# Routing inside the next batch's attention steps, wide reciprocals on VectorE, and an earlier split of the expert input

## What is computed

```
mod = silu(c) @ wmod                       # sa, ca, ga, sb, cb, gb for each batch
h = layernorm(x) * (1 + ca) + sa
x = x + ga * attention(h, W_qkv, W_out)    # causal, rotary, softmax(q k / 8) v
h = layernorm(x) * (1 + cb) + sb
w = softmax(h @ gate_w.T + expert_bias)    # the two largest, divided by their sum
y = sum over the two experts e of w_e * gelu(h @ w_up[e].T) @ w_down[e].T
x = x + gb * (layernorm(y) + h)
```

## Time and profile before

| | |
|---|---|
| median of 3 runs | 1188.57 us (1187.76 to 1191.32) |
| the profiled execution: time, span | 1190.89 us, 1188.6 us |
| attention, first to last output of a step | 94.3 to 829.1 us |
| routing, last attention write to first expert matmul | 829.8 to 962.5 us |
| experts | 962.5 to 1131.7 us |
| PE, DVE, ACT, POOL busy | 82%, 75%, 58%, 50% of the span |

### The profile page before, as it was taken

How to read it: one execution, slowest core, us unless ns; L and a number is a source line. 1 busy time by engine, 2 the same in 40 slices (tenths; PEclk the granted TensorE clock), 3 DMA queues, 4 the chain that set the end, 5 groups by cost and what they waited for, 6 DMA issues and landing times. The chain is left out here.

```text
span 1188.6 us, 21528 instructions
## 1 busy us (share of the span) xinstructions
PE 975.8 (82%) x6216; PEld 697.0 (59%) x6216; DVE 890.0 (75%) x1759; ACT 685.3 (58%) x1741; POOL 591.3 (50%) x436
## 2 busy tenths in 40 slices
PE   2369999999999999999999999997465169999910
PEld 1246666666676666667666766765465147777700
DVE  6547888788888888888888878885778149877717
ACT  2236776767677777767776767765311046666604
POOL 2334555555555555545555545552177706655530
PEclk9999999999999999999999999999555579999965
DMA  6222222222212222222212222220211455555424
GB/s 195 57 51 62 50 63 55 59 58 53 67 44 66 49 62 56 56 62 49 66 45 66 51 60 58 53 54 5 107 53 50 137 192 209 209 202 210 161 69 148
DMA packets 62971, 101.64 MB, mean 86 GB/s; under 512 B 10987, under 2 KB 45688, under 8 KB 59312
## 3 DMA queue, kind: packets, MB, share of 16 engines
q1 hardware_dynamic: 56944, 89.61, 26.3%
q0 software_dynamic: 4992, 8.94, 2.2%
q10 hardware_dynamic: 960, 2.33, 0.5%
HBM read 21.09 MB, written 15.50 MB: 31 GB/s over the span
## 5 line engine op out<-in xcount | busy, mean ns | idle before, releaser
L553 ACT ACTIVATE prob<-ps,nmax 128x512 f32<-128x512 f32 (+3 forms) x512 | 266.6, 526 | 71.6 <-DVE nmax L642 59.8
L724 POOL TENSOR_TENSOR qk<-tt,ur 128x1024 f32<-128x1024 f32 x64 | 151.7, 2371 | 217.2 <-DMA ur<-uu 195.1
L642 DVE TENSOR_REDUCE nmax<-ps 128x2 f32<-128x1024 f32 (+3 forms) x256 | 211.1, 825 | 8.8
L479 PE MATMUL ps<-ident,prob 128*128 128x128 f32 x1280 | 193.2, 281 | 7.5 <-ACT probt L574 3.7
L728 POOL TENSOR_TENSOR qk_lo<-qk,qk_hi 128x1024 fp32r<-128x1024 f32 x64 | 153.0, 2391 | 81.6 <-ACT qk_hi L581 81.6
L574 ACT COPY probt<-ps 128x512 f32<-128x512 f32 (+2 forms) x256 | 123.8, 511 | 97.0 <-PE ps L479 95.8
L479 PEld LDWEIGHTS ps<-ident,prob 128*128 128x128 f32 x1280 | 145.1, 142 | 53.8 <-ACT probt L574 24.1
L501 PE MATMUL ps<-probt,val 128*64 128x512 f32 (+3 forms) x1024 | 152.4, 440 | 0.0
L635 DVE TENSOR_TENSOR ps<-ps,tri 128x256 f32<-128x256 f32 x256 | 109.5, 428 | 51.2 <-PE ps L458 51.2
L1336 POOL DMA_INDIRECT results<-y,to_i x92 | 101.5, 1104 | 91.7 <-DVE y L1237 70.1
L622 DVE TENSOR_TENSOR uu<-ps,turn_s 128x1024 f32<-128x1024 f32 x64 | 78.4, 1225 | 57.2 <-PE ps L423 57.1
(11 more groups left out here) (204 smaller groups left out, 2281.4 us busy)
## 6 DMA issues: line engine op xcount, KB each, us to landing
ur<-uu SPq DMA_DIRECT2D x256, 128.0 KB, 2.3
wt<-wall SPq DMA_DIRECT2D x23, 1024.0 KB, 4.7
xg<-slots SPq DMA_DIRECT2D x23, 288.0 KB, 3.7
hb<-h_hi SPq DMA_DIRECT2D x64, 64.0 KB, 1.9
hb<-h_lo SPq DMA_DIRECT2D x64, 64.0 KB, 1.9
y<-results SPq DMA_DIRECT2D x8, 512.0 KB, 6.8
slots<-fill SPq DMA_DIRECT2D x8, 288.0 KB, 2.7
x_all<-in_x SPq DMA_DIRECT2D x4, 512.0 KB, 10.7
```

The source lines that it names most:

```text
L479: mm = e.transpose(ps[:, PT + at % 2, at_block * P:(at_block + 1) * P], prob[:, unit, kk * P:(kk + 1) * P], ident[:])
L553: e.activation(prob[:, unit, 0:w], ps[:, bank_s(idx) + j, 0:w], ACT.Exp, bias=nmax[:, q.par, idx, j:j + 1], accum_out=den[:, q.par, 2 * i ...
L642: e.tensor_reduce(nmax[:, q.par, idx, :], ps[:, bank:bank + 2, 0:w], AX.X, ALU.max, negate=True).then_inc(v_max, 1)
L724: e.tensor_tensor(qk[:], tt[:], ur[:], op=ALU.add).then_inc(g_qk, 1)
```

## The change

1. **Routing moves into attention.** Batch b's statistics are taken in slot 4 of the next batch's steps, its normalisation in slots 6 and 7, logits and choice in slots 0 to 4 of the batch after that, and its 8 scatters go out on POOL in slots 5, 6 and 7. The row buffer `rows` holds one batch, and `r_rows` of a batch waits for all scatters of the batches before it. What is left at the end is in `LATE`: the last twelve slots' routing.
2. **`dve_rden` writes the spread reciprocals itself**, 128x512 out of a broadcast 128x8; `pool_rep` and `rrep` are gone. `pe_turn_sum` stands ahead of the second scores, and `3a` behind the third.
3. **The loop over batches is written out** (68 slots).
4. **Weights**: all four loads are asked for after attention, into two buffers, the last two behind the 8 fills and each behind the split of the buffer's earlier content; the first expert weights wait for all four.
5. **Experts**: `pe_x` comes at group 0, `act_x` and `dve_x` at group 1.

```diff
+        def r_stats(e, b):
+            e.wait_ge(v_acc, HP * (b + 1))
+            if due(b):
+                e.wait_ge(r_fac, b)
+            for t in range(TB):
+                e.bn_stats(st4[:, t, :], x_all[:, b * TB + t, :]).then_inc(r_st, 1)
...
+        def r_factors(e, b, half):
+            t0, t1, t2, less, rstd4, minus = (f4[:, i, :] for i in range(6))
+            done, tick = r_f, Count(12 * b + 8 * half)
+            if half == 0:
+                e.wait_ge(r_st, TB * (b + 1))
+                e.tensor_tensor(t0, st4[:, :, 1], st4[:, :, 4], op=ALU.subtract).then_inc(done, 1)
...
+            e.tensor_tensor(t2, t1, numbers[:, MINUS_HALF, 0:TB], op=ALU.pow).then_inc(done, 1)
...
+        def r_norm(e, b):
+            e.wait_ge(r_fac, b + 1)
+            if due(b):
+                e.wait_ge(p_x1, b)
+            for t in range(TB):
+                ins = e.activation(xh2[:, t, :], x_all[:, b * TB + t, :], ACT.Identity, bias=f4[:, 5, t:t + 1],
+                                   scale=f4[:, 4, t:t + 1])
+            ins.then_inc(r_xh, 1)
...
+        def r_rows(e, b):
+            e.wait_ge(p_x2, b + 1)
+            if due(b):
+                e.wait_ge(d_xs, 16 * 2 * TB * b)
+                e.wait_ge(d_h2, 16 * b)
+            e.copy(rows[:, :, 0:E], ps[:, BANK_R, :].rearrange("p (t f) -> p t f", t=TB)).then_inc(r_row, 1)
...
+        def r_scatter(e, b, first_, last):
+            if first_ == 0:
+                e.wait_ge(r_slot, b + 1)
+                e.wait_ge(r_row, b + 1)
+                e.wait_ge(r_tail, b + 1)
+            for k in range(first_, last):
+                e.indirect_dma_start(xs, bass.IndirectOffsetOnAxis(slots[:, k // 2, k % 2:k % 2 + 1], 0),
+                                     rows[:, k // 2, :], None).then_inc(d_xs, 16)
...
+        def spare_read(e, i, c):
+            i, c = (i, c) if c >= 0 else (i - 1, 7)
+            if c == 7 and batch(i, 1) is not None:
+                e.wait_ge(r_ht, batch(i, 1) + 1)
+            b = batch(i, 2)
+            if b is not None:
+                if c == 0:
+                    e.wait_ge(r_row, b + 1)
+                elif c == 1:
+                    e.wait_ge(r_first, b + 1)
+                elif c == 4:
+                    e.wait_ge(r_base, b + 2)
+        def route_pe(e, i, c):
+            b, a = batch(i, 2), batch(i, 1)
+            if c == 0 and b is not None:
+                r_back(e, b)
+            if c == 1 and b is not None:
+                r_logits(e, b)
+            if c == 4 and b is not None:
+                r_places(e, b)
+            if c == 7 and a is not None:
+                r_features(e, a)
+        def route_act(e, i, c):
+            b, a = batch(i, 2), batch(i, 1)
+            if c == 0 and b is not None:
+                r_rows(e, b)
+            if c == 1 and b is not None:
+                r_exp(e, b)
+            if c == 6 and a is not None:
+                r_norm(e, a)
+            if c == 7 and a is not None:
+                r_shift(e, a)
+        def route_dve_first(e, i, c):
+            a = batch(i, 1)
+            if c == 4 and a is not None:
+                r_stats(e, a)
+        def route_dve(e, i, c):
+            b = batch(i, 2)
+            if b is None:
+                return
+            if c == 1:
+                r_best(e, b)
+            if c == 2:
+                r_one(e, b)
+            if c == 3:
+                r_two(e, b)
+            if c == 4:
+                r_slots(e, b)
+        def route_pool(e, i, c):
+            b, a = batch(i, 2), batch(i, 1)
+            if c in (4, 5) and a is not None:
+                r_factors(e, a, c - 4)
+            if c >= 5 and b is not None:
+                r_scatter(e, b, *((0, 2), (2, 5), (5, 8))[c - 5])
+        def route_sp(e, i, c):
+            b = batch(i, 2)
+            if c == 1 and b is not None:
+                r_keep(e, b)
...
             def pe_slot(e, i, c):
-                q0, q1, q2, v = Pair(i, c - 2), Pair(i, c - 3), Pair(i, c - 4), Tile(i, c)
+                (q0, q1, q2), v = pairs(i, c), Tile(8 * i + c)
                 if q0.live:
                     pe_qk(e, q0)
                 if q2.live:
+                    spare_read(e, i, c - 1)
                     pe_turn_prob(e, q2, "0")
                     pe_turn_prob(e, q2, "2a")
                 if q1.live:
...
                 if q2.live:
                     pe_turn_prob(e, q2, "2b")
                     pe_turn_prob(e, q2, "1")
+                    pe_turn_sum(e, q2)
                 if q1.live:
                     pe_scores(e, q1, 1)
                 if q2.live:
-                    pe_turn_sum(e, q2)
                     pe_values(e, q2)
                 if q1.live:
+                    pe_scores(e, q1, 2)
                     pe_turn_prob(e, q1, "3a")
-                    pe_scores(e, q1, 2)
                 if q2.live:
                     pe_out(e, q2)
                 if q1.live:
                     pe_turn_prob(e, q1, "3b")
                 if v.live:
                     pe_v(e, v)
+                if c in SPARE:
+                    if q1.live:
+                        e.wait_ge(a_ev, 4 * q1.n + 1)
+                    elif q2.live:
+                        e.wait_ge(v_ev, 2 * q2.n + 2)
+                    route_pe(e, i, c)
                 if q1.live:
                     pe_scores(e, q1, 3)
...
                     act_exp(e, q1, 0)
                     act_exp(e, q1, 1)
-                    act_store(e, q1, "3a")
                     act_exp(e, q1, 2)
                     act_exp(e, q1, 3)
+                    act_store(e, q1, "3a")
                 if q0.live:
                     act_hi(e, q0)
                 if q1.live:
                     act_exp(e, q1, 4)
+                route_act(e, i, c)
                 if v.live:
                     act_v(e, v)
...
             def dve_rden(e, q):
                 e.wait_ge(a_exp, NU * (q.n + 1))
                 if due(q.n):
-                    e.wait_ge(g_rep, q.n)
-                e.reciprocal(rden[:], den[:, q.par, :]).then_inc(v_rden, 1)
+                    e.wait_ge(p_r, q.n)
+                e.reciprocal(rden[:].rearrange("p t j f -> p (t j) f"),
+                             den[:, q.par, :].unsqueeze(2).to_broadcast([P, NU, HD])).then_inc(v_rden, 1)
...
-                q0, q1, q2 = Pair(i, c - 2), Pair(i, c - 3), Pair(i, c - 4)
+                q0, q1, q2 = pairs(i, c)
+                route_dve_first(e, i, c)
                 if q2.live:
                     dve_mask(e, q2, 3)
                     dve_max(e, q2, 3)
...
-            def pool_rep(e, q):
-                e.wait_ge(v_rden, q.n + 1)
-                if due(q.n):
-                    e.wait_ge(p_r, q.n)
-                e.tensor_tensor(rrep[:].rearrange("p t j f -> p (t j) f"),
-                                rden[:].unsqueeze(2).to_broadcast([P, NU, HD]),
-                                ones[:].unsqueeze(2).to_broadcast([P, NU, HD]), op=ALU.mult).then_inc(g_rep, 1)
...
             def all_slots(e, slot):
-                for c in range(8):
-                    slot(e, 0, c)
-                with e.Fori(1, B) as i:
-                    for c in range(8):
-                        slot(e, i, c)
-                for c in range(4):
-                    slot(e, B, c)
+                for n in range(STEPS + 4):
...
-                    e.dma_start(w_raw[:], w_up[:, 0:WH]).then_inc(d_e[0], 16)
                     all_slots(e, sp_slot)
...
+                    for q in range(4):
+                        if q >= 2:
+                            e.wait_ge(s_wlo, q - 1)
+                        e.dma_start(raw[q % 2][:], (w_up, w_down)[q // 2][:, q % 2 * WH:(q % 2 + 1) * WH]).then_inc(d_e[q], 16)
+                        if q == 1:
+                            for i, c in LATE:
+                                route_sp(e, i, c)
+                            e.wait_ge(v_ended, 1)
+                            for x in range(NX):
+                                end = e.value_load(ended[0:1, x:x + 1], min_val=x * REGION, max_val=x * REGION + B * S)
+                                e.dma_start(xs[bass.ds(end, S), :].rearrange("(p t) f -> p t f", t=TB),
+                                            fill[:].unsqueeze(1).to_broadcast([P, TB, ROW])).then_inc(d_fill, 16)
+                    e.wait_ge(v_table, 1)
                     for j in range(NTL):
                         col = e.value_load(table[0:1, 0, j:j + 1], min_val=0, max_val=(NX - 1) * 4 * I)
...
                                     xs[bass.ds(row, S), :].rearrange("(p t) f -> p (t f)", t=TB)).then_inc(d_xg[j % 3], 16)
+                        if j == 0:
+                            e.wait_ge(s_wlo, 4)
                         if due(j - 2):
...
-                            if g % IC == 1 and g // IC + 1 < NTL:
+                            if g % IC == 0 and g // IC + 1 < NTL:
                                 pe_x(e, g // IC + 1)
...
+                    for i, c in LATE:
```

(25 more changed lines are left out.)

562 lines of the change are left out of this document (255 added, 307 removed).

## The result

The changed kernel takes 1482.38 us (median of 4 runs, 1482.16 to 1484.43), the kernel before 1188.94 (4 runs, 1187.76 to 1191.32): a ratio of 1.247, 95% interval 1.245 to 1.249. The forecast was 1460 us, range 1335 to 1540.

What follows compares the result with a forecast made beforehand. The prediction took the loop between PE and DVE in attention to set the pace: 63 x (16.6 - 11.66) = +311, routing +44, behind attention -70, experts -10, start -3.5, together +271, hence 1460 us, range 1335 to 1540.

Steps and rivals of the forecast that it cites:

- The reciprocal: In attention's loop, dve_rden at 512 elements takes 3.62 us, 3.54 start to start, at 6.8 ns an element from three widths.
- The rival of eight plain operations: A wide reciprocal costs eight plain operations, up to 10.4 ns an element, 5.4 us: 1573 us in all; chance 0.02.
- The clock: PE's idle time ahead of pe_turn_sum lowers TensorE's clock in most attention steps: 1.4 us a step, making 16.6.
- a chance of 0.04: Rival: each attention step starts slow as long as the experts do, losing 2.9 us a step, 1554 us; chance 0.04.
- the loop itself: The loop between PE and DVE in attention, with the wide reciprocal at a steady clock: 15.2 us a step.
- Routing inside the steps: Routing moved into attention's steps adds 6.8 us a batch, 4.1 of it on PE, for some 6.5 batches: +44 us.
- the rival of 1173 us: The reciprocal does not scale: a wide one costs 0.68 us like any operation, total 1173 us, faster; chance 0.12.
- Behind attention: The routing chain left between attention and the experts falls from 132.7 to 63 us: -70 (-60 to -75).
- Experts: Between expert tiles, the earlier dve_x removes 0.54 us idle 22 times: -10 us (0 to -15).
- Start: At attention's start PE's first input no longer queues behind a 1 MB load: -3.5 us (0 to -5).
- The written-out loop: Writing the batch loop out gives at most 11.66 - 11.41 a step, nothing where the DVE loop sets the pace.
- What would show it: Marks if right: dve_rden 3.4 to 3.8 us, PE idle 3.5 or more, steps 16 to 17, routing remainder 57 to 73.

Runs made afterwards that it cites:

- e2: The kernel before with the wide reciprocal alone (dve_rden writes 128x512, pool_rep gone): 1532.3 us, ratio 1.281.
- e3: The changed kernel, but VectorE makes the reciprocal narrow (128x8) and then copies it out to 128x512: 1240.3 us, ratio 1.036.
- e4: The changed kernel with 12 unused 512-column matmuls added on PE in the idle time ahead of pe_turn_sum: 1380.1 us, ratio 1.154.
- e8: The changed kernel, wide reciprocal kept, with the routing's pieces on VectorE, ScalarE and GpSimd placed as in e6: 1448.5 us, ratio 1.211.
- e12: The changed kernel with only VectorE's routing pieces (r_stats, r_one, r_two) moved ahead of dve_ot: 1441.9 us, ratio 1.209.
- e1: The changed kernel with the narrow reciprocal (128x8) on VectorE and the spreading back on GpSimd: 1268.2 us, ratio 1.060.
- e6: e1 with PE's order of before and the routing's pieces on VectorE, ScalarE and GpSimd moved within their slots: 1192.7 us, ratio 0.997.
- e7: The kernel before with the experts' part alone (pe_x at group 0, act_x and dve_x at group 1): 1183.2 us, ratio 0.988.
- e11: e7 with the loop over batches written out: 1183.1 us, ratio 0.995.

## Why the prediction was right, and where it was not

**The mechanism was right.** A loop between PE and DVE that the wide reciprocal lengthens, and a clock that falls in PE's idle time: e2 has it alone, e3 takes away the rate, e4 takes away only the clock. The forecast's step of 16.6 us was 17.1.

**The reciprocal**: 3.345 us for a forecast 3.62, 3.26 from start to start for 3.54, so 6.25 ns an element above the narrow one and not 6.8. The sum was 18 us too high here (63 x 0.28). The three widths did not lie on one line as I said: between the two widest of the earlier trace rows the slope is 0.05 us for 8 elements, 6.3 ns, and that is what was measured. The rival of eight plain operations took 10.4 ns for one element; e3's copy does 512 in 0.432 us, and eight of those are 3.46. The repeat count of 8 of the Trainium skill ("VectorE: DVE Perf Modes", First, the fixed hardware budget) fits this trace within 4%, as an estimate, when the plain element is that of the copy. My rival failed by pricing it from `L1399`.

**The clock** is the term that was mis-sized. I took 1.4 us a step from the one fall that I saw among attention's steps, 2.40 us at half clock. In the step shown it is 5.58 us of work at 0.50, which loses 2.8 us, of which 2.4 show in the step (17.1 for e4's 14.7): 63 x 1.0 = 63 us more. The stretch is near the 5.80 us behind attention, a length that I gave a chance of 0.04. I had also misread the row of 2.40 us. It was cut there by me, and the fall goes on: the mean clock of the 5.00 us behind it is 0.89. And attention has a second fall, behind a piece of 1.31 us idle where I had argued that 1.30 us does nothing (PE was busy 1.20 us of the 2.86 before the fall):

```profile
795.00:797.86 2.86, 1.20 (x8) 0.69 (x8) 2.03 (x4) 2.73 (x11) 2.74 (x2) 1.00 0.11 26
797.86:801.27 3.41, 3.41 (x19) 2.39 (x15) 2.00 (x4) 0.59 (x1) 1.68 (x3) 0.50 0.57 132
824.10:829.10 5.00, 4.04 (x25) 2.16 (x24) 0.73 (x2) 0.58 (x1) 0.00 (x0) 0.89 0.00 0
```

Together with the loop itself (14.7 at a steady clock for a forecast 15.2, -32) this makes the step 0.5 us longer than forecast: +33.

**Routing inside the steps**: forecast +44, measured +33: 1112.6 us from the first to the last output, less 63 x 17.13. The size is near, the reason was wrong. Of 6.8 us a batch I gave 4.1 to PE; e8 and e12 keep all of PE's work and lose nothing. The 6.4 us of a middle batch are DVE's pieces at the end of slots 2 and 3 and at the start of 4: in e12 the interval that ends in slot 3 falls from 19.6 to 16.3 us and the one that ends in slot 4 from 20.7 to 17.1. I had given DVE about 2 us, and missed that an operation of `r_one` (L350) and the first of `r_two` (L369) wait for GpSimd, 1.7 to 1.8 us each:

```profile
498.43 2.40 POOL L1035 TENSOR_TENSOR qk_lo<-qk,qk_hi 128x1024 fp32r<-128x1024 f32 x1 [6.89 <-ACT qk_hi L892]
498.92 1.96 DVE L369 TENSOR_TENSOR tied<-tied,rank 128x32 f32<-128x32 f32 x1
```

```profile
L350 DVE SCALAR_TENSOR_TENSOR tied<-expo,rank x8: 180/1866/1866, 335.8 to 1234.6; 128x32 f32<-128x32 f32 x8
L369 DVE TENSOR_TENSOR tied<-tied,rank x8: 183/1958/1959, 355.4 to 1236.0; 128x32 f32<-128x32 f32 x8
```

L369 ends at 500.88, POOL's operation at 500.83; in the last batch, with POOL idle, L369 takes 0.183 us. After e12's move, with the code of the operation unchanged, the median of its eight is 0.180. The Trainium skill ("SBUF — State Buffer", SBUF: two separate sides) calls the port pair of the two engines "an exclusive lock" for a VectorE operation with two SBUF inputs beside a GpSimd operation that reads SBUF; the trace agrees. And the small price held only beside the wide reciprocal: at a fast step the same routing costs 21 to 27 us a batch (e1), which no step of the prediction foresaw. The +33 is a difference and holds more than routing: with routing inside, most stretches of work at half clock last 3.4 us and two in each batch 7.2 to 7.7, in place of 5.3 to 6.0, so that the clock's part changes too. The runs do not separate the two. Had the reciprocal not scaled, as in the rival of 1173 us, the kernel would not have been faster: e3 is nearly that kernel and has a ratio of 1.036. That rival, with its price of 34 us for routing, was some 60 us too low, and the 0.11 for faster had no case behind it.

**Behind attention**: 64.0 us left for a forecast 63. The chain and its order were right.

**Experts**: forecast -10 (0 to -15), measured -19.2, outside the range of this term. I priced the labelled idle time of 0.54 us. From start to start the gap is 0.93 us where back-to-back matmuls have 0.23, so 0.70 was to be had; after, the same place has 0.31:

```profile
1297.13 0.39 PE L1231 MATMUL ps<-hh,wt 128*128 128x512 f32 x1
1297.44 0.47 PE L1218 MATMUL ps<-xt_hi,wt 128*128 128x512 f32 x1
```

That is 0.62 of the 0.87 us gained on each of 22 tiles (nearly all 7.2 to 7.4 us before, 6.4 to 6.5 after); the other 0.25 was not traced. I also shaved the gain for DVE being nearly full, and it was not needed.

**Start**: PE's first input comes 3.2 us earlier (52.66 for 55.82), as forecast (-3.5), but the first output does not: the first step through the wide reciprocal takes it back. In e1, e3 and e6 the first output is at 90.3, 91.5 and 90.7.

**The written-out loop**: I put it at nothing or a small gain. Beside the wide reciprocal it is nothing (137.0 us for eight steps, 136.7 in e2 with the loop); in a fast loop it is a loss, 8 us by the ratios of e7 and e11.

**What would show it**: the marks were met or missed narrowly. `dve_rden` at 3.35 us (3.4 to 3.8 named), PE idle 3.39 us ahead of L792 (3.5 or more), released by DVE, plain steps of 16.3 to 17.5 us (16 to 17), half-clock matmuls behind the idle time, 64 us behind attention (57 to 73).

The terms' errors, +33 for the step, -11 for routing, -9 for the experts, +1 behind, +4 at the start and +1 at the end, add up to +20 before rounding, which is what the two spans differ by beyond the forecast (291.7 for 271.5). That the total came so near is in part luck: the clock's +63 is half paid back by the loop's -32, and the rest by routing and the experts, where the reason or the size was wrong.

## What to carry to other kernels

Price an operation in a loop between two engines by the whole loop, and by what the wait does to TensorE's clock: here 3.26 us of reciprocal cost 5.5 us a step though neither engine was full. Compute a reciprocal on the narrow tile and spread it with a copy. When work is moved into another stage's steps, ask on each engine what stands behind it in the queue, and not only how much idle time the engine has: the same pieces cost 21 to 27 us a batch, 5 to 9 us or nothing, by place and by what was slow beside them. Where a change brings several edits, try them alone: the fastest kernel here keeps four of this change's five parts, with the routing's pieces rearranged.
